# Turning filtered pieces to tokens with whole 128x128 transposes, and sorting chunks in the copies out

## The chip, the cores and the metric

The kernel runs on one core of one Trainium2 chip. The metric is the device time of one execution, in microseconds. The matrix engine (TensorE, PE in the profile) multiplies into eight PSUM banks of 2 KB per partition; ScalarE (ACT) and VectorE (DVE) read those banks; GpSimd (POOL) works on SBUF alone; SyncE (SP) only starts transfers here.

## The reference

The reference is one decoder layer: an attention-like block, a second block on the context, and a feed-forward block, each with a residual and a layer norm. The change lies in the first block, in two causal depthwise filters over the value stream, with 31 and 64 taps:

```python
v = jax.nn.silu(_dwconv_causal(hidden_states @ v_w.T, convv_w))
def fir(x, filt):
    y = _dwconv_causal(x.reshape(b, Ll, H * DV), filt.reshape(H * DV, -1))
    return y.reshape(b, Ll, H, DV)
short, long_, wide = (fir(v, fir_s), fir(v, fir_l), fir(v, fir_wd))
...
o = w_ctx[..., 0:1] * short + w_ctx[..., 1:2] * long_ + w_ctx[..., 2:3] * wide + w_ctx[..., 3:4] * delta_out + w_val * v
```

There are 4 sequences of 512 tokens and 256 channels. `delta_out` is a chunked delta rule: a 128x128 triangular inverse for each 128 tokens and two heads, then a recurrence over the four tiles of tokens. Everything is float32 in this part.

## The kernel before

The program is five stages, one after another. **Stage 2**, from 59.9 us to about 344.5 us of the profiled span, has the keys and queries, the inverse, the recurrence and both long filters. It is written by hand, engine by engine: each engine has its own queue in the order of the code, and waits for counters (semaphores) that the others raise.

**The filters** go over the 256 channels in 32 pieces of 8 channels. For one piece n:

- POOL copies the piece's values into `v_piece` (L1448).
- `filter_piece(n)` (L732) does 8 matmuls on PE, one for each channel: the values of 32 chunks (4 sequences of 8 chunks of 64 tokens) against a 128x128 table that holds both filters' taps. Two channel groups of 4 fill columns 0 to 255 of the piece's bank: partition = (channel of 4, chunk of 32), column = (filter, token of 64).
- ACT copies the bank's left half to SBUF, into `fir_s`, with the tokens turned round (`filter_out`, L1081, signal `windows_out`).
- `to_tokens(n)` (L745) brings tokens onto the partitions, on PE, with the result in columns 256 to 511 of the same bank.
- ACT copies that to `filtered` (`tokens_out`, L1086, signal `fir_out`), whose layout is partition = token within a tile of 128, then (filter, tile of 16, channel of 256). A piece has 8 neighbouring channels, so one tile is 1 KB from the next.

A tile of 128 tokens is two chunks: the one of even number belongs on partitions 0 to 63, the one of odd number on 64 to 127. Before the change `to_tokens` does this sorting itself: the constant `c_select` (128x128) picks the 16 tiles' even or odd chunks, in 8 small matmuls, for two groups of channels, two filters and two parities. One copy of 128x256 then suffices.

**Order around it.** PE runs `to_tokens(n - 1)` behind the 8 matmuls of `filter_piece(n)`. ACT's `filter_out(n)` is `tokens_out(n - 1)` and then the copy of piece n. `filter_piece(n + 1)` waits for the copy of piece n (`windows_out`) and for `fir_out` of piece n - 1. Pieces 0 to 7 lie in the **opening** of stage 2 (62 to 97 us), in one bank and between the steps that prepare sequence 0. After it, for each sequence b, comes `inverse(b)` (five rounds of products, no filter work) and `recurrence(b)`: seven pieces each for b = 0, 1, 2 (p0 to p6 below), three for b = 3. In `recurrence(b)` PE weaves the pieces between the steps of the recurrence and those that prepare sequence b + 1:

- turn_k (L756), updates (L692), next_state (L949), outputs (L967), piece p0, q_norms (L765), piece p1, turn_norms (L771)
- state_part (L927), p2, updates, p3, next_state, outputs (L964, L967)
- state_part, p4, updates, turn_back (L779), next_state, outputs, p5
- state_part, p6, updates, gram (L795, L799), to_tokens(p6), outputs; then `attend` (L819) opens `inverse(b + 1)` and waits for `fir_out` of p6.

ACT has in the same stretch, between its copies for pieces, `u_out` (L1154: PE's next_state waits for it), `square` (L1065), `k_back_out` (L1117: PE's gram waits for it) and `cross_out` (L1124).

Of the kernel before, what the change touches and what calls it, by code (L numbers as in the profile page):

```python
# [24 lines left out]
P = 128  # L25
B, L, D = 4, 512, 256
H, DK = 4, 64
# [3 lines left out]
NJ = L // DK  # L31
# [8 lines left out]
PIECE = 8  # L40
# [8 lines left out]
def shape_constants():  # L49

    i = np.arange(P)
    c = {}
    c["ident"] = np.eye(P)
    row, col = i[:, None] % DK, i[None, :] % DK
# [11 lines left out]
    for m in range(KT):  # L66
        heads[i, m, 12 + 2 * m + i // DK] = 1.0
    c["heads"] = heads
    sel = np.zeros((4, B, NJ, 2, 4, B, NJ // 2))
    for par in range(2):  # L70
        sel[:, :, par::2, par] = np.eye(4 * B * (NJ // 2)).reshape(4, B, NJ // 2, 4, B, NJ // 2)
    c["select"] = sel
    t = np.arange(HALF)
    f = np.arange(P)
    dft, inv = np.zeros((HALF, 4, P)), np.zeros((P, 4, HALF))
# [91 lines left out]
def layer(nc, dr, out):  # L167
    ctx = ExitStack()
    with ctx:
        def sb(name, shape, dt=F32):  # L170
            return ctx.enter_context(nc.sbuf_tensor(name, shape, dt))
# [16 lines left out]
        arena = sb("arena", [P, 30624])  # L188

        const_shapes = {n: a.shape[1] for n, a in shape_constants().items() if n not in LATE_CONST}  # L190
        const = {n: sb("c_" + n, [P, w]) for n, w in const_shapes.items()}
        ident = const["ident"]
# [20 lines left out]
        def stat_of(b, n, s):  # L213
# [38 lines left out]
        filtered = arena[:, 0:WL].rearrange("p (f t c) -> p f t c", f=2, c=D)  # L252
# [3 lines left out]
        A2 = carve(arena, {  # L256
            "xT": (KT, L), "kq": (2, 4, L), "k_tok": (2, TT, D), "v_sc": (TT, D),
            "above": (TT, 2, KT, DK), "cross": (TT, 2, KT, DK), "atT": (TT, 2, KT, P), "X": (TT, 2, KT, DK),
            "XT": (TT, 2, P), "Z": (2, 2, 4, DK // 2), "full": (TT, 2, KT, P),
            "S": (2, KT, P), "ss": (32,), "ks": (16,), "C": (16,), "root": (TT, H), "rn": (2, 2 * TT, H), "th": (16,),  # L260
            "v_piece": (2, PIECE, B * NJ), "fir_s": (4, DK)},
            at=WL + TOEP_BUFS * TOEP)
# [349 lines left out]
        fir_bank = lambda n: bank[5 if n < OPENING else 3]  # L612
# [11 lines left out]
        half = lambda a: slice(a * DK, (a + 1) * DK)  # L624
# [30 lines left out]
        with nc.Block() as block:  # L655
# [30 lines left out]
            def _(pe):  # L686
                mm = nc.tensor.matmul
# [50 lines left out]
                def to_tokens(n):  # L738

                    pe.wait_ge(s2["windows_out"].sem, n + 1)  # L740
                    for c4 in range(PIECE // 4):
                        for f in range(2):
                            for par in range(2):
                                col = D + f * P + c4 * DK
                                i = mm(fir_bank(n)[half(par), col:col + DK], A2["fir_s"][:, 2 * c4 + f, :],  # L745
                                       const["select"][:, half(par)], start=True, stop=True)
                    i.then_inc(s2["turn_mm"].sem, 1)

                def turn_k(b):
# [222 lines left out]
                def recurrence(b, more):  # L972
# [19 lines left out]
                    if more:  # L992
                        filter_piece(piece[3])
                    else:
                        to_tokens(piece[2])
# [19 lines left out]
                    if more:  # L1015
                        gram(b + 1, 0)
                        gram(b + 1, 1)
                        to_tokens(piece[6])
# [30 lines left out]
            def _(act):  # L1049
# [33 lines left out]

                def tokens_out(n):
                    act.wait_ge(s2["turn_mm"].sem, n + 1)
                    nc.scalar.copy(filtered[:, :, :, n * PIECE:(n + 1) * PIECE].rearrange("p f t c -> p f c t"),  # L1086
                                   fir_bank(n)[:, D:2 * D].rearrange("p (f c t) -> p f c t", f=2, c=PIECE))\
                        .then_inc(s2["fir_out"].sem, 1)

                def beta_rows_out(b):  # L1090
                    act.wait_ge(s2["beta_rows"].sem, s2["beta_rows"].at(b, 1))
# [1555 lines left out]
```

## Time and profile before

| | us |
|---|---|
| median of 3 executions | 709.68 (709.62 to 709.91) |
| the profiled execution, its own time | 705.24 |
| its span, first to last instruction | 703.4 |
| mean granted clock of TensorE over the span | 0.944 of 2.4 GHz |

| engine | busy us | share | instructions |
|---|---|---|---|
| PE matmul | 585.3 | 83% | 7436 |
| PE weight load | 426.2 | 61% | 7448 |
| DVE | 455.5 | 65% | 890 |
| ACT | 282.8 | 40% | 518 |
| POOL | 118.5 | 17% | 102 |

Busy is the union of an engine's instructions in time. One float32 matmul stands in the trace as two records, one float32 transpose as one. Instructions of one engine overlap: the second can start before the first has ended, so the distance between two starts is what an instruction takes from its engine, and its own duration is what one who waits for it sees. The profiled execution was 4.4 us shorter than the median of the timed ones; the span and what lies around it are 705.24 us.

### The profile page before, as it was taken

How to read it: one execution, taken by the hardware profiler on the slowest of the kernel's cores; microseconds unless marked ns; L12 is line 12 of the kernel's file. 1: busy time of each engine (PE TensorE's matmuls, PEld its weight loads, DVE VectorE, ACT ScalarE, POOL GpSimd, SP SyncE). 2: the span in 40 equal slices, each digit the busy share in tenths (PEclk: the TensorE clock that was granted, in tenths of full speed). 3: DMA queues.
4: the chain of work that ended last, by engine and by line, in shares of the span. 5: the costliest groups of instructions: out<-in, count | busy, mean ns of one | idle time of the engine just before them, and what ended most of it. 6: DMA issues, size and time to landing. Idle time of an engine off the chain costs nothing. (4 is left out here: it accounts for less than half of the span.)

```text
span 703.4 us, 16960 instructions
## 1 busy us (share of the span) xinstructions
PE 585.3 (83%) x7436; PEld 426.2 (61%) x7448; DVE 455.5 (65%) x890; ACT 282.8 (40%) x518; POOL 118.5 (17%) x102
## 2 busy tenths in 40 slices
PE   5868679899998999878696886599999767998984
PEld 2544466777767676776443545488888554555542
DVE  2963367857784786774818889664277774676674
ACT  1874634432453344323344253332323144554431
POOL 1001340250034006000011203434100020000000
PEclk9999899999999999998799998899999887999998
DMA  5501420340052004001510005400000000000001
GB/s 175 207 1 44 152 79 4 104 139 4 4 156 89 3 23 161 4 4 64 207 31 30 31 0 156 134 1 0 1 1 0 1 0 1 1 0 31 31 4 58
DMA packets 26537, 37.51 MB, mean 53 GB/s; under 512 B 4641, under 2 KB 13602, under 8 KB 26463
## 3 DMA queue, kind: packets, MB, share of 16 engines
q1 hardware_dynamic: 26463, 36.42, 16.0%
q8 instruction: 59, 0.97, 0.6%
q14 instruction: 15, 0.12, 0.1%
HBM read 34.31 MB, written 2.10 MB: 52 GB/s over the span
## 5 line engine op out<-in xcount | busy, mean ns | idle before, releaser
L298 DVE SCALAR_TENSOR_TENSOR arena<-bank,conv_w,arena 128x511 f32<-128x511 f32 (+2 forms) x72 | 53.2, 746 | 30.9 <-ACT arena L1070 15.5
L1448 POOL COPY arena<-v_win 128x256 f32<-128x256 f32 x32 | 21.1, 684 | 196.8 <-PE bank L732 196.8
L1898 ACT COPY arena<-bank 128x512 f32<-128x512 f32 x40 | 23.3, 584 | 57.1 <-PE bank L1701 36.8
L1701 PE MATMUL bank<-v_win,arena 128*128 128x256 f32 x192 | 45.6, 386 | 0.0
L2473 PE MATMUL bank<-v_win,arena 128*128 128x256 bf16 x288 | 36.5, 279 | 7.9 <-DVE arena L2560 6.9
L732 PE MATMUL bank<-arena 128*32 128x128 f32 x512 | 35.7, 409 | 8.1 <-ACT arena L1081 7.6
L1131 ACT COPY arena<-bank 128x512 f32<-128x512 f32 x40 | 21.6, 589 | 50.8 <-PE bank L854 50.8
L1086 ACT COPY arena<-bank 128x256 f32<-128x256 f32 x32 | 19.3, 602 | 53.9 <-PE bank L745 53.9
L1701 PEld LDWEIGHTS bank<-v_win,arena 128*128 128x128 f32 x192 | 37.1, 195 | 5.5 <-issue 0.4
L2473 PEld LDWEIGHTS bank<-v_win,arena 128*128 128x128 bf16 x288 | 28.4, 100 | 16.6 <-DVE arena L2560 7.9
L2463 PE MATMUL bank<-arena,v_win 128*128 128x512 bf16 x134 | 35.1, 390 | 3.7 <-DVE arena L2531 3.2
L1683 PE MATMUL bank<-v_win,arena 128*128 128x256 f32 x128 | 31.9, 409 | 5.9 <-DVE arena L2165 4.0
L2463 PE MATMUL bank<-arena 128*128 128x512 bf16 x142 | 35.5, 385 | 0.1
L1627 PE MATMUL bank<-arena 128*128 128x512 f32 x64 | 33.4, 649 | 0.0
L1683 PEld LDWEIGHTS bank<-v_win,arena 128*128 128x128 f32 x128 | 26.2, 207 | 10.6 <-issue 4.2
L839 PE MATMUL bank<-arena 64*64 64x32 f32 x1280 | 23.5, 221 | 9.3 <-DVE arena L1344 3.9
L705 PE MATMUL bank<-arena,qkv_w 128*128 128x512 f32 x64 | 30.2, 597 | 0.9 <-PEq L303 0.6
L865 PEld LDWEIGHTS bank<-arena 64*64 64x64 f32 x1280 | 21.7, 139 | 11.6 <-issue 11.1
L839 PEld LDWEIGHTS bank<-arena 64*64 64x64 f32 x1280 | 20.9, 134 | 12.0 <-DVE arena L1344 7.1
L2510 ACT CAST arena<-arena 128x512 bf16<-128x512 f32 x24 | 14.8, 618 | 31.7 <-DVE arena L2540 31.7
L732 PEld LDWEIGHTS bank<-arena 128*32 128x32 f32 x512 | 15.8, 122 | 18.8 <-issue 13.5
L745 PEld LDWEIGHTS bank<-c_select,arena 128*64 128x64 f32 x512 | 18.3, 142 | 14.6 <-issue 12.9
(275 smaller groups left out, 1355.4 us busy)
## 6 DMA issues: line engine op xcount, KB each, us to landing
arena<-in_toep_w SPq DMA_DIRECT2D x32, 256.0 KB, 3.0
arena<-in_toep_l SPq DMA_DIRECT2D x32, 256.0 KB, 3.7
arena<-in_xT SPq DMA_DIRECT2D x12, 512.0 KB, 4.6
arena<-in_x SPq DMA_DIRECT2D x4, 512.0 KB, 3.9
arena<-in_ctx SPq DMA_DIRECT2D x4, 512.0 KB, 4.4
out<-arena SPq DMA_DIRECT2D x4, 512.0 KB, 2.9
qkv_w<-in_qkv_wT SPq DMA_DIRECT2D x1, 768.0 KB, 5.4
v_win<-in_w_gateT SPq DMA_DIRECT2D x1, 768.0 KB, 4.9
```

The lines of the kernel that those rows point to most:

```text
L298: return nc.vector.scalar_tensor_tensor(out=acc[:, j:L], in0=src[:, 0:L - j], scalar=conv_w[:, m, CONV_K - 1 - j:CONV_K - j], in1=acc[:, j:L],
L705: i = mm(proj_bank(m)[:], qkv_w[:, k, m * P:(m + 1) * P], A2["xT"][:, k, :], start=(k == 0), stop=(k == KT - 1))
L732: i = mm(fir_bank(n)[32 * (c % 4):32 * (c % 4) + 32, (c // 4) * P:(c // 4 + 1) * P], A2["v_piece"][:, n % 2, c, :], toep[n % TOEP_BUFS][:, ...
L839: i = mm(zw_bank(th, a)[half(p), c:c + DK // 2], A2["above"][half(a), t, e, p, :], x, start=True, stop=True)
L865: i = mm(zw_bank(th, p)[half(a), c:c + DK // 2], A2["XT"][half(p), t, e, half(a)], A2["Z"][half(p), th, a, 2 * t2 + e, :], start=True, sto ...
L1131: nc.scalar.copy(A2["XT"][:, 2 * th:2 * th + 2, :, :], turn_bank(th)[:].rearrange("p (t e c) -> p t e c", t=2, e=2)).then_inc(s2["xt_out"] ...
L1627: mm(hid_bank(m)[:], g1x_w[:, k, m * P:(m + 1) * P], A3[b % 2]["xT"][:, k, :], start=(k == 0), stop=False)
L1683: i = mm(o[:, par * 256:(par + 1) * 256], src[:, par, k, d * P:(d + 1) * P], dft[:, k, par * 256:(par + 1) * 256], start=(k == 0), stop=(k ...
L1701: i = mm(oo, src[:, k, f * P:(f + 1) * P], w[:, k, :], start=(k == 0), stop=(k == KT - 1 and f > 0))
L1898: nc.scalar.copy(dst(i), bank[RING_FIRST + n % RING].rearrange("p (t c) -> p t c", c=dst(i).shape[-1]))\
L2463: i = mm(bank[first + n % 2][:], w[:, k, m * P:(m + 1) * P], parts[b % 2][part][:, k, :], start=(j == 0 and k == 0), stop=(j == 2 and k == ...
L2473: i = mm(bank[6 + t // 2][:, (t % 2) * D:(t % 2 + 1) * D], parts[b % 2][part][:, m, t * P:(t + 1) * P], wd[:, m, :], start=(m == 0 and j = ...
```

## The change

`to_tokens` does two transposes for a piece instead of eight matmuls with `c_select`: one for each group of four channels, of the whole 128x128 window (both filters, 64 tokens each). Its result has partition = (filter, token of 64) and column = (channel, tile, parity). The constant is gone, with its load. `tokens_out` now does the sorting: for each filter and each parity one copy from 64 partitions of the bank to 64 partitions of `filtered`, 8 channels by 16 tiles each, reading every second column. Only the last of the four raises `fir_out`.

```diff
@@ shape_constants
-    sel = np.zeros((4, B, NJ, 2, 4, B, NJ // 2))
-    for par in range(2):
-        sel[:, :, par::2, par] = np.eye(4 * B * (NJ // 2)).reshape(4, B, NJ // 2, 4, B, NJ // 2)
-    c["select"] = sel
@@ to_tokens
                     for c4 in range(PIECE // 4):
-                        for f in range(2):
-                            for par in range(2):
-                                col = D + f * P + c4 * DK
-                                i = mm(fir_bank(n)[half(par), col:col + DK], A2["fir_s"][:, 2 * c4 + f, :],
-                                       const["select"][:, half(par)], start=True, stop=True)
+                        i = nc.tensor.transpose(fir_bank(n)[:, D + c4 * P:D + (c4 + 1) * P],
+                                                A2["fir_s"][:, 2 * c4:2 * c4 + 2, :].rearrange("p f t -> p (f t)"), ident[:])
                     i.then_inc(s2["turn_mm"].sem, 1)
@@ tokens_out
-                    nc.scalar.copy(filtered[:, :, :, n * PIECE:(n + 1) * PIECE].rearrange("p f t c -> p f c t"),
-                                   fir_bank(n)[:, D:2 * D].rearrange("p (f c t) -> p f c t", f=2, c=PIECE))\
-                        .then_inc(s2["fir_out"].sem, 1)
+                    turned = fir_bank(n)[:, D:2 * D].rearrange("p (c t two) -> p c t two", c=PIECE, two=2)
+                    for f in range(2):
+                        for par in range(2):
+                            i = nc.scalar.copy(filtered[half(par), f, :, n * PIECE:(n + 1) * PIECE].rearrange("p t c -> p c t"),
+                                               turned[half(f), :, :, par])
+                    i.then_inc(s2["fir_out"].sem, 1)
```

No instruction changes its place in a queue; SP loses one transfer, and DVE and POOL keep their instructions. Lines after L69 have moved up, by 4 to 7 ahead of `tokens_out` and by 4 behind it. PE at the end of the opening, before: `filter_piece(6)`, its turn of piece 5 (L745), `filter_piece(7)`, the turns of pieces 6 and 7, and `attend` (L819).

```order
L732 MATMUL bank<-arena 32x128 x8
L745 MATMUL bank<-c_select,arena 64x64 x8
L732 MATMUL bank<-arena 32x128 x8
L745 MATMUL bank<-c_select,arena 64x64 x16
L819 MATMUL bank<-arena 128x128 x8
```

The same place on PE after, where L728 is the filter, L738 the turn and L812 `attend`:

```order
L728 MATMUL bank<-arena 32x128 x8
L738 MATMUL bank<-c_ident,arena 128x128 x2
L728 MATMUL bank<-arena 32x128 x8
L738 MATMUL bank<-c_ident,arena 128x128 x4
L812 MATMUL bank<-arena 128x128 x8
```

Each turn of a piece went from eight matmuls to two transposes, at the same places. ACT in `recurrence(0)`, before, from the turned piece p1 (L1086) to the copies of the scaled keys (L1117):

```order
L1086 COPY arena<-bank 128x2x8x16
L1081 COPY arena<-bank 128x256
L1154 COPY arena<-bank 128x256
L1086 COPY arena<-bank 128x2x8x16
L1081 COPY arena<-bank 128x256
L1065 ACTIVATE arena<-arena 128x1024
L1086 COPY arena<-bank 128x2x8x16
L1081 COPY arena<-bank 128x256
L1154 COPY arena<-bank 128x256
L1117 COPY arena<-bank 128x2x256 x2
```

The same place on ACT after; L1082 is the copy of the turned piece, L1074 that of the filtered one, L1150 is `u_out`, L1058 `square` and L1113 `k_back_out`:

```order
L1082 COPY arena<-bank 64x8x16 x4
L1074 COPY arena<-bank 128x256
L1150 COPY arena<-bank 128x256
L1082 COPY arena<-bank 64x8x16 x4
L1074 COPY arena<-bank 128x256
L1058 ACTIVATE arena<-arena 128x1024
L1082 COPY arena<-bank 64x8x16 x4
L1074 COPY arena<-bank 128x256
L1150 COPY arena<-bank 128x256
L1113 COPY arena<-bank 128x2x256 x2
```

Every copy of a turned piece became four in a row, of half the partitions and half the elements for each partition; what stands behind each is the same as before.

## Rows read from the trace of the kernel before

**Rows 1.** Group by line and shape, 80 to 420 us: busy us, mean ns, idle before.

```profile
L1086 ACT COPY arena<-bank 128x256 f32<-128x256 f32 x29 | 17.5, 603 | 51.9 <-PE bank L745 51.9
```

**Rows 2.** Groups of ACT by line and shape, whole span, same columns.

```profile
L1154 ACT COPY arena<-bank 128x256 f32<-128x256 f32 x16 | 6.0, 373 | 8.4 <-PE bank L692 8.4
...
L1124 ACT COPY arena<-bank 64x512 f32<-64x512 f32 x8 | 4.6, 577 | 12.6 <-DVE arena L1281 12.6
...
L482 ACT COPY arena<-bank 128x128 f32<-128x128 f32 x4 | 1.1, 265 | 3.6 <-PE bank L400 3.6
```

**Rows 3.** Timeline of ACT in stage 1: start us, duration us, instruction.

```profile
43.57 0.27 ACT L482 COPY arena<-bank 128x128 f32<-128x128 f32 x1
43.73 0.64 ACT L450 ACTIVATE arena<-arena 128x512 f32<-128x512 f32 x1
```

**Rows 4.** Timeline of all engines in `recurrence(1)`, around piece p3's turn.

```profile
209.45 0.69 PE L745 MATMUL bank<-c_select,arena 128*64 128x64 f32 x16
...
209.96 0.64 PE L692 MATMUL bank<-arena 128*64 128x64 f32 x16
210.18 0.63 ACT L1086 COPY arena<-bank 128x256 f32<-128x256 f32 x1 [2.32 <-PE bank L745]
...
210.53 1.09 PE L779 MATMUL bank<-c_ident,arena 128*128 128x128 f32 x8
210.60 0.42 ACT L1081 COPY arena<-bank 128x256 f32<-128x256 f32 x1
210.91 0.38 ACT L1154 COPY arena<-bank 128x256 f32<-128x256 f32 x1
...
211.46 0.61 PE L949 MATMUL bank<-arena 128*128 128x128 f32 x4
```

**Rows 5.** The same timeline: pieces p2, p3 and p6, then the end.

```profile
201.47 1.11 PE L732 MATMUL bank<-arena 128*32 128x128 f32 x16 [0.40 <-ACT arena L1081]
...
204.32 1.11 PE L732 MATMUL bank<-arena 128*32 128x128 f32 x16 [0.65 <-ACT arena L1081]
...
216.13 1.11 PE L732 MATMUL bank<-arena 128*32 128x128 f32 x16 [0.47 <-ACT arena L1081]
...
221.93 0.60 ACT L1086 COPY arena<-bank 128x256 f32<-128x256 f32 x1 [0.58 <-PE bank L745]
...
223.29 1.16 PE L819 MATMUL bank<-arena 64*128 64x128 f32 x16
```

**Rows 6.** Timeline of PE in the opening, where it waits for ACT.

```profile
80.40 1.08 PE L765 MATMUL bank<-arena,c_heads 128*32 128x128 f32 x16 [4.84 <-ACT arena L1112]
...
84.53 1.14 PE L732 MATMUL bank<-arena 128*32 128x128 f32 x16 [0.70 <-ACT arena L1081]
...
92.55 1.11 PE L732 MATMUL bank<-arena 128*32 128x128 f32 x16 [1.11 <-ACT arena L1081]
...
95.19 0.69 PE L745 MATMUL bank<-c_select,arena 128*64 128x64 f32 x16 [0.91 <-ACT arena L1081]
...
96.76 1.16 PE L819 MATMUL bank<-arena 64*128 64x128 f32 x16 [0.89 <-ACT arena L1086]
```

**Rows 7.** Timeline of PE in `recurrence(3)`, pieces p2 and its turn.

```profile
328.42 1.11 PE L732 MATMUL bank<-arena 128*32 128x128 f32 x16 [0.47 <-ACT arena L1081]
...
331.05 0.69 PE L745 MATMUL bank<-c_select,arena 128*64 128x64 f32 x16 [0.44 <-ACT arena L1081]
```

**Rows 8.** Windows: us, busy PE, PEld, DVE, ACT, POOL; clock; DMA share, GB/s.

```profile
40.00:48.00 8.00, 5.96 (x64) 4.67 (x54) 6.85 (x11) 6.10 (x15) 0.00 (x0) 1.00 0.01 2
...
94.00:96.00 2.00, 0.96 (x26) 0.68 (x22) 0.22 (x1) 1.37 (x4) 1.19 (x2) 1.00 0.58 150
78.00:80.00 2.00, 0.00 (x0) 0.00 (x0) 0.00 (x0) 2.00 (x6) 2.00 (x1) 0.50 0.87 294
```

**Rows 9.** Timeline of PE in `inverse(3)`, in a stretch of half clock.

```profile
305.18 1.16 PE L865 MATMUL bank<-arena 64*64 64x32 f32 x64 [0.33 <-ACT arena L1131]
...
310.90 1.93 PE L865 MATMUL bank<-arena 64*64 64x32 f32 x64
```

## The prediction

> **What bounds the kernel now.** The busy table is the first view: PE 83%, ACT 40%. That alone would say that a lighter PE and a heavier ACT must pay. But the turns of pieces stand only in stage 2's opening and recurrences, so I read who waits there, in the timeline. There PE is often the one that waits, and it waits for ACT: `filter_piece` for the copy of the piece before it by 0.40, 0.65 and 0.47 us in one recurrence [rows 5], by 0.70 and 1.11 us in the opening, where the turns themselves and `attend` wait for ACT too, by 0.91 and 0.89 us [rows 6], and in the last recurrence [rows 7]. Between these waits PE runs without a gap, and ACT waits for PE: 51.9 us in 29 waits before the copy of the turned piece [rows 1]. So this is a ring. PE's turn, ACT's copy of the turn, ACT's copy of the next piece, PE's next filter; each piece goes once round it. What counts is what the change takes from PE's part of the ring and what it adds to ACT's, not the shares.
>
> **PE's part, removed.** A turn takes 0.51 us from PE (209.45 to the next group's 209.96), and ACT starts its copy 0.73 us after the turn's start (210.18) [rows 4]. Whole transposes are in the same row group: the eight of L779 take from 210.53 to 211.46, 0.93 us, 0.117 each, and the first start to the last end is 1.09, so the last one lasts 0.27. Two take 0.23 us from PE and end after 0.117 + 0.27 = 0.39; ACT starts 0.04 behind the end of a turn now (210.18 against 209.45 + 0.69), so 0.43 after the start. **PE's next work is 0.28 us earlier, ACT's copy 0.30 us.**
>
> **ACT's part, added.** The one copy of 128x256 lasts 0.603 us [rows 1]; a plain copy of that shape lasts 0.373, one of 128x128 lasts 0.265 [rows 2]. That is 0.84 ns for each element of a partition and 0.157 fixed. The other 0.23 us, 0.9 ns per element, must come from its writes, each 1 KB from the last, since its reads are plain. The next copy starts 0.40-0.42 after it and ends late too: 0.42 against 0.38 for the L1154 behind it [rows 4]. The four new copies write in the same way, 128 elements each, together 512 elements for each lane where there were 256. Half the partitions save nothing: 64x512 lasts 0.577 [rows 2], on the line of 0.157 + 512 x 0.84 = 0.587.
>
> What the four cost ACT is not in the trace, so I bound it. Let **x** be the time by which everything behind them on ACT comes later, counted from their start. From below: a plain 128x128 copy lets the next begin after 0.16 us [rows 3]; four are 0.64, against 0.40 now: x = 0.24. Below zero is excluded, because twice the elements per lane can't be copied in less. From above: four without any overlap, each 0.265 + 128 x 0.9 ns = 0.38, are 1.52: x = 1.12. The nearest rows lie between. Twice the present pace, four times 0.20 us, gives x = 0.40. The write pace, 512 elements at 1.73 ns against 256, gives 0.44, and with three joints of 0.04 (0.16 less 128 x 0.84 ns is 0.05) 0.56. I take **x = 0.48**, the middle of 0.40 and 0.56, because both are the same scattered writes. `fir_out` comes 3 x 0.22 + 0.38 = 1.04 after the start, where it was 0.60: 0.44 later, less the 0.30.
>
> What no row shows is the read of every second column. By the Trainium skill's SBUF page ("SBUF — State Buffer", Door 1: The DMA port swizzle) PSUM is read in lines of 8 bytes and SBUF in lines of 16, and each change of line is paid for. The reversed read of L1081 costs little; a step of 8 bytes is not in the trace. If that read were the slower side, the case is the first rival below.
>
> **The opening, pieces 0 to 7.** Each term is followed to the place where PE waits. ACT reaches the copies of q's squares, for which PE waits 4.84 us, as a row of its own work: the copies for pieces 1 and 2 lie in it, once with PE ahead by 0.58 and a wait of 0.16 us on PE absorbed: 2x - 0.74 = +0.22. The turn behind that is at half clock and saves about 0.45; F(5) waits for the next copy: 3x - 1.19 = +0.25. Then each piece adds x - 0.30 = 0.18: F(6) and the grams ahead of it +0.43, F(7) +0.61, the last turn +0.79. `attend` waits for the turned piece's copy: 0.79 - 0.30 + 0.44 = 0.93. **Opening: +0.9 us.** The wait behind each of these is already ACT's [rows 6], so nothing covers them.
>
> **A recurrence of seven pieces.** p2's filter waits for ACT: x - 0.30 = +0.18. p3's: +0.36. next_state behind p2's turn is PE's own pace again: 0.36 - 0.28 = +0.08. p3's turn: `u_out` comes 0.08 - 0.30 + 0.48 = +0.26 later, and next_state starts at 211.46, some 0.11 us after it needs to (210.91 + 0.38 and 0.06 to react [rows 4]): +0.15. p5's filter follows, p6's waits for ACT: 0.15 - 0.30 + 0.48 = +0.33. Then two turns on PE with no wait for ACT between them, updates and grams behind the first and outputs behind the second: 0.33 - 0.28 - 0.28 = -0.23. `attend` waits for the last copy, which ended at 222.53, 0.76 before `attend` started [rows 5]; it ends 0.05 - 0.30 + 0.44 = +0.19 later, still hidden. **-0.23 us each, -0.7 in three.** Without the cover of those 0.76 us it would be +0.19. In general one is 4x - 2.15, so it turns from gain to loss at x = 0.54. The DVE work that opens the next inverse waits for the outputs and goes with them.
>
> **The last recurrence.** Two waits for ACT [rows 7], the first turn at half clock: (x - 0.45) + (x - 0.30) - 0.28 = **-0.1**; after it DVE's reductions follow the outputs. The missing 64 KB load lies among the first loads, whose data are not needed until later: nothing. Stages 3 to 5 start when stage 2 ends, so its shift is the kernel's.
>
> **Sum:** +0.9 - 0.7 - 0.1 = +0.1 us. On the profiled execution, 705.24, that is 705.4; on the median of the timed runs, which is 4.4 us more throughout, 709.68 + 0.1 = **709.8 us**. The sum is about 21x - 10 (7x from the opening, 12x from three recurrences, 2x from the last), so 0.1 us of x is 2.1 us of time. 0.2% is 1.4 us, about what a measurement of this kernel can tell from no change.
>
> **Rivals.**
>
> 1. *ACT takes over the ring: slower.* If the strided read, or a pause between copies, makes x over 0.55, every wait of PE for ACT grows and PE's savings are only idle time. For it: ACT already ends the wait at four places of the opening and three of each recurrence [rows 5, 6]. Against it: overlapping is what every pair of ACT rows shows. At x = 0.65 it is 21 x 0.17 = +3.6: **713.4**. At the upper bound of 1.12 it would be 13 us. Chance 0.28.
>
> 2. *The scattered writes hide in the overlap: faster.* Four copies at the plain pace with a little more, x = 0.30, give -3.8: **705.9**. For it: the next copy starts 0.20 us before the scattered one ends. Against it: that next copy ends late. Chance 0.22.
>
> 3. *The clock falls.* The granted clock fell to half (1.2 GHz) when PE had stood idle from 75.6 us on [rows 6, 8]; at 94 to 96 us PE is busy for 0.96 of 2 us and it holds. There PE will stand longer. If it fell there, the first products of `inverse(0)` would run at 1.93 instead of 1.16 us for a group of 64 records [rows 9]; two such and the transposes beside them are about 2 us: **711.9**. Chance 0.07. By the Trainium skill ("TensorE: Matmul & The Clock Gate", Part 4: PE-mode transpose) a transpose does not count as busy for the clock, which would make this likelier. The trace speaks against it: from 40 to 48 us most of PE's records are stage 1's transposes of the values, and the clock is 1.00 [rows 8].
>
> That the change doesn't do what it says can be left out: the order of both engines shows the new instructions at the old places.
>
> **How the numbers follow.** My forecast, within 1.4 us of before, has 0.43; the rivals 0.28, 0.22 and 0.07. The range reaches from x = 0.34 (-3.0) to x = 0.68 (+4.2): **706.7 to 713.9**. Faster by over 0.2% 0.22, within it 0.43, slower 0.35.
>
> **What would show it.** Two records of about 0.27 us per turn, and ACT's copy 0.43 us behind the turn's start: PE's part right. ACT's starts from the first of four to the copy of the next piece: 0.88 is x = 0.48; over 0.95 is rival 1, under 0.75 rival 2. Start of `attend` in the opening later by 0.9; a recurrence, from its first updates to `attend`, shorter by 0.2. PE's waits for L1074 larger than those for L1081 were, each by about 0.2 more than the one before. The forecast is wrong altogether if the copies' durations differ from 0.38 by much, or if the stretches at half clock lie elsewhere than at 78 to 85, 310 to 313 and 320 to 327 us.

## The result, and the profile after

| | us | before, measured beside it |
|---|---|---|
| median of 4 executions | 720.53 (717.49 to 725.77) | 709.65 (709.34 to 709.91) |
| the profiled execution | 725.77 | 705.24 |
| its span | 724.0 | 703.4 |
| mean granted clock | 0.924 | 0.944 |

The ratio is 1.0161, with a 95% interval of 1.0099 to 1.0223: the change made the kernel slower by 1.0 to 2.2%, 10.9 us by the medians. The forecast was 709.8, with a range to 713.9. It is the case that the prediction had at the upper bound of its first rival, 13 us.

The page of the kernel after, busy time of each engine:

```profile
PE 589.3 (81%) x7000; PEld 423.6 (59%) x7000; DVE 455.6 (63%) x890; ACT 315.7 (44%) x614; POOL 118.5 (16%) x102
```

ACT has 33 us more, PE 4 us more with 436 fewer records (more of its time at half clock). Both together say little about 20 us of span. The page's groups of instructions say more; the columns are busy us, mean ns of one, idle time before them and what ended it:

```profile
L1082 ACT COPY arena<-bank 64x128 f32<-64x128 f32 x128 | 47.9, 374 | 44.4 <-PE bank L738 43.3
...
L728 PE MATMUL bank<-arena 128*32 128x128 f32 x512 | 35.7, 409 | 22.4 <-ACT arena L1074 21.9
```

The copy of a turned piece was one of 603 ns [rows 1]; it is four of 374 ns. And the filter (L728) now waits 21.9 us for the copy of the piece before it. In the kernel before, the list of PE's waits has 7.6 us for the same pair of lines:

```profile
PE bank L732 <- ACT arena L1081: 7.6, 13, 1.1
```

The same list of the kernel after (us in total, times, longest):

```profile
PE bank L728 <- ACT arena L1074: 21.9, 14, 2.2
...
PE bank L758 <- ACT arena L1108: 6.2, 1, 6.2
...
PE bank L812 <- ACT arena L1082: 4.5, 4, 1.8
PE bank L942 <- ACT arena L1150: 4.4, 8, 0.7
```

`attend` (L812) waited once for the turned piece before the change, 0.89 us [rows 6]; now it waits in front of each of the four inverses. next_state (L942) waits for `u_out` eight times, 4.4 us, where it waited five times, 2.4 us. The number of the filter's waits is nearly the same, 14 against 13. They are three times as long: no new wait arose there, the old one grew.

The timeline of PE and ACT in `recurrence(1)` after, at full clock, pieces p2 to p4 (start us, duration us, instruction, idle time before it):

```profile
219.53 1.11 PE L728 MATMUL bank<-arena 128*32 128x128 f32 x16 [1.50 <-ACT arena L1074]
220.57 0.44 PE L738 MATMUL bank<-c_ident,arena 128*128 128x128 f32 x2
...
220.94 0.69 PE L688 MATMUL bank<-arena 128*64 128x64 f32 x16
221.05 1.52 ACT L1082 COPY arena<-bank 64x128 f32<-64x128 f32 x4 [0.81 <-PE bank L738]
222.60 0.37 ACT L1074 COPY arena<-bank 128x256 f32<-128x256 f32 x1
222.87 0.38 ACT L1150 COPY arena<-bank 128x256 f32<-128x256 f32 x1
223.22 1.11 PE L728 MATMUL bank<-arena 128*32 128x128 f32 x16 [1.60 <-ACT arena L1074]
```

Read it as the ring of the prediction. PE's turn starts at 220.57, ACT's four copies at 221.05. They take until 222.57. The copy of the next piece starts at 222.60, 1.55 us after the first of the four. It was 0.42 us after it before (210.18 to 210.60, [rows 4]). PE's next filter follows at 223.22. Between the four copies there is no overlap at all: 4 x 0.374 is 1.50, and the row's 1.52 to 1.56 us is that with a few ns between each two. Record by record, each of the four starts about 12 ns after the end of the one before, and the copy behind them 24 ns after. By the prediction's measure, x = 1.17 (1.57, the usual distance, less 0.40).

**Where the time went, part by part.** I cut each profiled span at the first product of stage 2 on PE, at the starts of `attend`, and at the first updates of each recurrence. `inverse` is from `attend` to the first updates, `recurrence` from there to the next `attend`, the last one to VectorE's first instruction of stage 3. All in us; in brackets how much of it had the clock at half.

| part | before | after | e3, one copy | e2, runs | e7, before + runs |
|---|---|---|---|---|---|
| stage 1 | 59.9 (3.4) | 63.1 (10.2) | 62.4 (10.2) | 57.7 (0) | 62.0 (6.8) |
| opening | 36.9 (6.8) | 45.0 (19.8) | 34.8 (6.8) | 39.6 (13.7) | 35.9 (6.8) |
| inverse(0) | 33.5 (0) | 36.9 (7.5) | 35.0 (3.4) | 36.6 (6.8) | 33.5 (0) |
| recurrence(0) | 29.4 | 32.9 (3.4) | 26.5 | 29.4 | 27.7 |
| inverse(1) | 34.5 | 33.5 | 34.3 | 33.8 | 34.5 |
| recurrence(1) | 29.1 | 31.8 | 26.5 | 29.4 | 28.9 |
| inverse(2) | 34.5 | 33.5 | 34.3 | 33.8 | 34.5 |
| recurrence(2) | 28.2 | 32.9 (3.4) | 26.5 | 29.4 | 27.7 |
| inverse(3) | 33.5 (3.4) | 30.0 (0) | 30.4 | 29.9 | 33.1 (3.4) |
| recurrence(3) | 25.1 (10.6) | 25.9 (7.6) | 22.7 (7.3) | 23.8 (3.9) | 23.2 (3.4) |
| the rest | 358.9 | 358.5 | 358.7 | 358.7 | 358.1 |

The three right columns are experiments, told below. From before to after: opening +8.1, inverse(0) +3.4, the recurrences +3.5, +2.7, +4.7 and +0.8, inverse(3) -3.5. Stage 1, whose instructions are the same in both, has +3.2: its stretches at half clock differ from one execution to the next. The profiled execution was also the slowest of the four.

The opening has a second cause beside the ring. Windows of the kernel after (columns as in [rows 8], the clock is the number after the busy times):

```profile
81.00:88.00 7.00, 2.39 (x34) 1.78 (x35) 1.00 (x6) 4.49 (x10) 3.80 (x3) 0.53 0.37 116
...
92.00:98.00 6.00, 5.21 (x105) 4.80 (x103) 1.44 (x3) 2.84 (x7) 5.92 (x3) 0.50 0.27 90
...
102.00:115.00 13.00, 9.22 (x118) 7.36 (x117) 2.05 (x5) 5.04 (x13) 0.62 (x1) 0.50 0.13 47
```

Before, the clock was at half for 6.8 us of the opening and at full through `inverse(0)`. Now it falls to half (1.2 GHz) three times, each time after PE has stood for ACT. The rows in front of the falls, PE's timeline:

```profile
85.61 1.08 PE L758 MATMUL bank<-arena,c_heads 128*32 128x128 f32 x16 [6.23 <-ACT arena L1108]
...
90.42 1.11 PE L728 MATMUL bank<-arena 128*32 128x128 f32 x16 [2.01 <-ACT arena L1074]
...
101.87 0.44 PE L728 MATMUL bank<-arena 128*32 128x128 f32 x4 [2.24 <-ACT arena L1074]
```

### The profile page after: what moved, and what is told of

The parts are those of the page before. It is cut to its first block and busy times, and to the rows that moved or that the text cites. A ratio compares the mean times of both kernels' runs of the same rounds, so it can differ in the third digit from the quotient of the medians.

```text
span 724.0 us, 16171 instructions
## 1 busy us (share of the span) xinstructions
PE 589.3 (81%) x7000; PEld 423.6 (59%) x7000; DVE 455.6 (63%) x890; ACT 315.7 (44%) x614; POOL 118.5 (16%) x102
## 5 line engine op out<-in xcount | busy, mean ns | idle before, releaser
L1082 ACT COPY arena<-bank 64x128 f32<-64x128 f32 x128 | 47.9, 374 | 44.4 <-PE bank L738 43.3
L728 PE MATMUL bank<-arena 128*32 128x128 f32 x512 | 35.7, 409 | 22.4 <-ACT arena L1074 21.9
L1894 ACT COPY arena<-bank 128x512 f32<-128x512 f32 x40 | 23.3, 585 | 56.9 <-PE bank L1697 36.7
L1679 PE MATMUL bank<-v_win,arena 128*128 128x256 f32 x128 | 31.8, 408 | 6.1 <-DVE arena L2161 4.1
L728 PEld LDWEIGHTS bank<-arena 128*32 128x32 f32 x512 | 15.9, 122 | 33.4 <-issue 28.3
L701 PE MATMUL bank<-arena,qkv_w 128*128 128x512 f32 x64 | 30.1, 595 | 0.9 <-PEq L299 0.6
L2506 ACT CAST arena<-arena 128x512 bf16<-128x512 f32 x24 | 14.8, 618 | 31.6 <-DVE arena L2536 31.6
L354 PE MATMUL bank<-arena,qkv_w 128*128 128x512 f32 x32 | 19.5, 753 | 9.8 <-DMA c_ident<-in_c_ident 7.6
```

Of the source, the lines that this page charges most:

```text
L701: i = mm(proj_bank(m)[:], qkv_w[:, k, m * P:(m + 1) * P], A2["xT"][:, k, :], start=(k == 0), stop=(k == KT - 1))
L728: i = mm(fir_bank(n)[32 * (c % 4):32 * (c % 4) + 32, (c // 4) * P:(c // 4 + 1) * P], A2["v_piece"][:, n % 2, c, :], toep[n % TOEP_BUFS][:, ...
L1082: i = nc.scalar.copy(filtered[half(par), f, :, n * PIECE:(n + 1) * PIECE].rearrange("p t c -> p c t"), turned[half(f), :, :, par])
L1679: i = mm(o[:, par * 256:(par + 1) * 256], src[:, par, k, d * P:(d + 1) * P], dft[:, k, par * 256:(par + 1) * 256], start=(k == 0), stop=(k ...
L1894: nc.scalar.copy(dst(i), bank[RING_FIRST + n % RING].rearrange("p (t c) -> p t c", c=dst(i).shape[-1]))\
L2506: nc.scalar.copy(parts[u]["h_hi"][:, m, :], A5[u]["h"][:, m % 2, :]).then_inc(s5["h_split"].sem, 1)
```

## The experiments

The four copies differ from the one in several ways at once: they read every second column, they write in the same scattered way but twice as many elements per lane, and they go from one partition half to another. So three theories on why x is 1.17 stood beside each other. **Read**: the step in the bank costs. **Write**: the scattered writes cost, 1 KB apart. **Half**: a copy on other partitions than the one before it can't begin until that one has ended. What each predicts stands in the quoted text of each experiment. The ratio given is to the kernel before, measured beside it. Each kernel's profile is of one execution.

**e1: contiguous reads.** POOL puts even and odd chunks apart in `v_piece`, so the turned columns of a parity lie side by side (POOL's side of the edit is left out here):

```diff
-turned = fir_bank(n)[:, D:2 * D].rearrange("p (c t two) -> p c t two", c=PIECE, two=2)
+turned = fir_bank(n)[:, D:2 * D].rearrange("p (c two t) -> p c two t", c=PIECE, two=2)
```

> The changed kernel with one thing else: GpSimd writes the 32 chunks of a channel in the order (parity, tile) instead of (tile, parity), so that each of ScalarE's four copies reads 16 neighbouring columns of the bank and not every second one. Same result, same four copies, same scattered writes. Theory R (the read of every second column keeps the copies from overlapping): the four starts move from 0.385 us apart to about 0.2, the distance from the first to the copy of the next piece from 1.57 to about 0.9 us, the time from 720.5 to about 710. Theory W (the writes, 1 KB apart, do it) and theory I (four instructions on half the partitions, whatever they read, do it): 1.57 us and about 720 as before.

721.93 us, ratio 1.0195 (1.014 to 1.0251), not told apart from the change itself; 14.8 us over before by the medians. The group of the four copies, in e1:

```profile
L1082 ACT COPY arena<-bank 64x128 f32<-64x128 f32 x128 | 47.9, 374 | 44.8 <-PE bank L738 43.7
```

47.9 us and 374 ns, to the digit what it was. The read step costs nothing, and the theory of the read falls. The prediction had weighed it by the Trainium skill ("SBUF — State Buffer", Door 1: The DMA port swizzle: PSUM read in lines of 8 bytes, each change of line paid for): for ACT's copies out of PSUM these runs show no such price at a step of 8 bytes.

**e2: writes in runs.** The same four copies with the loops of the copy exchanged. It writes the 8 channels of a tile side by side and reads them 128 bytes apart:

```diff
-i = nc.scalar.copy(filtered[half(par), f, :, n * PIECE:(n + 1) * PIECE].rearrange("p t c -> p c t"),
-                   turned[half(f), :, :, par])
+i = nc.scalar.copy(filtered[half(par), f, :, n * PIECE:(n + 1) * PIECE],
+                   turned[half(f), :, :, par].rearrange("p c t -> p t c"))
```

> The changed kernel with each of the four copies going over its elements in the other order: channel innermost, so that it writes runs of 8 neighbouring values (32 bytes) and reads with a step of 32 columns (128 bytes). Same result. Theory W: a copy takes 0.27 us instead of 0.37 and the next begins after 0.16 to 0.2; the distance from the first to the next piece's copy falls to 0.65 to 0.85 us, the time to 704 to 710. Theory R: the reads are as strided as before, 1.57 us and about 720 stay. Theory I: starts stay as far apart as a copy lasts, whatever that is; with 0.27 us a copy 1.1 us and about 713.

706.54 us, ratio 0.9989 (0.9959 to 1.0018). The order of two loops is worth 15 us here, against e1, measured beside it. Group, and one place in e2's timeline of ACT:

```profile
L1082 ACT COPY arena<-bank 64x128 f32<-64x128 f32 x128 | 33.3, 260 | 43.6 <-PE bank L738 42.5
```

```profile
221.74 1.08 ACT L1082 COPY arena<-bank 64x128 f32<-64x128 f32 x4 [1.77 <-PE bank L738]
222.84 0.37 ACT L1074 COPY arena<-bank 128x256 f32<-128x256 f32 x1
```

A copy takes 260 ns, the 265 of a plain one [rows 2]; 114 ns for 128 elements is 0.9 ns each, the prediction's figure. The writes are the price, and reads 128 bytes apart cost nothing either. But the four still don't overlap: 4 x 0.260 = 1.04 in 1.08, and the next after 1.10. After a plain copy of 128x128 the next instruction began 0.16 us later [rows 3]. So more than half of the trouble is left: x = 0.70.

**e3: one copy.** Transposes on PE as in the change, and one copy of the old shape. It leaves out the sorting of chunks into partition halves.

> The changed kernel's two transposes a piece, but ScalarE's one copy of 128x256 of the kernel before; the sorting of chunks into the partition halves is left out. It prices the TensorE part alone. By the prediction's sum, with x = 0: 21 x 0 - 10, about 700; the ring model of the prediction gives at least -5 us. If TensorE's part were idle time in any case (the rival that PE gains nothing): 709 to 710.

695.23 us, ratio 0.9837 (0.9798 to 0.9876). Timeline of ACT in `recurrence(1)` of e3:

```profile
207.84 0.63 ACT L1079 COPY arena<-bank 128x256 f32<-128x256 f32 x1 [1.87 <-PE bank L738]
208.26 0.44 ACT L1074 COPY arena<-bank 128x256 f32<-128x256 f32 x1
```

0.42 between the starts, as before. This is x = 0, where the prediction's sum says -10 us; the run says -11.9 (3.1 of it in `inverse(3)`, which the sum does not hold and which comes below). So PE's transposes bring about what was counted for them, and all that is lost is lost in the copies.

**e9: two full copies.** The same amount of scattered writing on all 128 partitions, in two copies of 128x128; it leaves out the layout that the later steps need.

```diff
-for f in range(2):
-    for par in range(2):
...
+for par in range(2):
+    i = nc.scalar.copy(filtered[:, par, :, n * PIECE:(n + 1) * PIECE].rearrange("p t c -> p c t"),
+                       turned[:, :, :, par])
```

> The changed kernel with two copies of all 128 partitions and 128 elements each (one for each parity) in place of four of 64 partitions; the move between partition halves is left out, so chunks of both parities lie in the wrong place. Reads of every second column and scattered writes stay. Theory H (half the partitions is what stops the overlap): the second starts about 0.2 to 0.3 us after the first, and the next piece's copy some 0.4 to 0.5 us after it starts; x is about 0.0 to 0.1 and the time about 697. Theory N (ScalarE copies with scattered writes of 128 elements don't overlap whatever their partitions): 0.385 us apart, 0.77 to the next piece's copy, x = 0.37, about 702.

693.67 us (one execution; before 708.46). ACT in `recurrence(1)` of e9:

```profile
214.16 0.62 ACT L1081 COPY arena<-bank 128x128 f32<-128x128 f32 x2 [1.78 <-PE bank L738]
214.56 0.42 ACT L1074 COPY arena<-bank 128x256 f32<-128x256 f32 x1
```

The two are 405 ns each by their group (64 of them), together 0.81, and lie in 0.62 us; the next starts 0.40 after the first. So splitting a copy costs nothing, scattered writes overlap well, and reading every second column changes nothing. What is left is the half.

**e4: four copies, old matmuls.** The kernel before with its one copy split in four, each from one half to the same half, the filter in the outer loop:

```diff
+turned = fir_bank(n)[:, D:2 * D].rearrange("p (f c t) -> p f c t", f=2, c=PIECE)
+for f in range(2):
+    for par in range(2):
+        i = nc.scalar.copy(filtered[half(par), f, :, n * PIECE:(n + 1) * PIECE].rearrange("p t c -> p c t"),
+                           turned[half(par), f, :, :])
```

> The kernel before, with its eight matmuls, but its one copy of 128x256 cut into four of 64x128: for each filter and each partition half, from a half to the same half, 16 neighbouring columns at a time, writes scattered as before. Same result. It prices the four copies alone. Theory R: starts about 0.2 us apart, 0.9 us to the next piece's copy, about 8 to 10 us slower than before (718 to 720). Theory W: 0.37 to 0.385 us apart, 1.57 us, 730 or more. Theory I: the same as W. Against each other W and I are told apart by the run with writes in runs.

734.81 us, ratio 1.0385 (1.0341 to 1.0428). 373 ns each, 12 ns between them: the change's copies without the transposes, and the worst kernel of all. Its `recurrence(1)` is 33.9 us against 31.8 after: PE's part of the ring is worth 2.1 us there, and was forecast as 2.15.

**e5: the same, half by half.** Only the two loops are exchanged, so two neighbouring copies have the same half:

```diff
-for f in range(2):
-    for par in range(2):
+for par in range(2):
+    for f in range(2):
```

> The run with the old matmuls and four copies of 64x128, with the copies in another order: both filters of the lower partition half first, then both of the upper, so that the first and second, and the third and fourth, stay on one half. Theory H1 (a copy on half the partitions never lets the next begin before it ends): all starts 0.385 us apart, as with the other order, median about 735. Theory H2 (only a change of the half between two copies stops the overlap): the first and third distance fall to about 0.2 us, the other stays, the group gets 0.35 us shorter and the time about 7 us.

728.51 us (one execution). Group and timeline of ACT in e5:

```profile
L1089 ACT COPY arena<-bank 64x128 f32<-64x128 f32 x128 | 38.0, 395 | 50.1 <-PE bank L745 49.8
```

```profile
218.41 1.19 ACT L1089 COPY arena<-bank 64x128 f32<-64x128 f32 x4 [1.07 <-PE bank L745]
219.63 0.37 ACT L1081 COPY arena<-bank 128x256 f32<-128x256 f32 x1
```

Four of 0.395 are 1.58, and they take 1.19: the two pairs overlap by 0.2 us each, and at the change of half there is a pause of 12 ns. The same four shapes, the same writes, only in another order. This settles the theory of the half, by the distances in the trace; the time, of one execution, agrees with it. The copy of all 128 partitions behind them also waits for the end (219.60 to 219.63).

**e7: the kernel before, with writes in runs.** If the writes cost 0.9 ns per element, the old kernel pays too:

```diff
-nc.scalar.copy(filtered[:, :, :, n * PIECE:(n + 1) * PIECE].rearrange("p f t c -> p f c t"),
-               fir_bank(n)[:, D:2 * D].rearrange("p (f c t) -> p f c t", f=2, c=PIECE))\
+nc.scalar.copy(filtered[:, :, :, n * PIECE:(n + 1) * PIECE],
+               fir_bank(n)[:, D:2 * D].rearrange("p (f c t) -> p f t c", f=2, c=PIECE))\
```

> The kernel before, with its one copy of the turned piece going channel by channel innermost, so that it writes runs of 8 values (32 bytes) and reads with a step of 64 bytes. Same result. Theory W for the scattered write: the copy lasts 0.37 to 0.38 us instead of 0.60 and the next piece's copy starts after 0.31 instead of 0.40, x = -0.09; by the ring model about 1.5 to 2 us less than before. If a copy's reads with a step cost as much as its writes do: no change.

703.56 us, ratio 0.9941 (0.991 to 0.9973): faster than both kernels. The group in e7, to be held against [rows 1]:

```profile
L1086 ACT COPY arena<-bank 128x256 f32<-128x256 f32 x32 | 11.9, 372 | 53.3 <-PE bank L745 53.3
```

603 ns became 372, the next copy starts 0.27 instead of 0.40 us later, and PE's wait for L1081 falls from 7.6 to 4.2 us. The gain is small for a copy 231 ns shorter, since the scattered writes were already overlapped by 0.2 us.

**e8: e2 with two banks in the opening.** The turns of pieces 0 to 7 go to a bank of their own (bank 4, unused there), and ACT copies the filtered piece ahead of the turned one. PE then doesn't wait for the four copies in its next filter; the next turn waits for them in its place:

```diff
+tok_bank = lambda n: bank[4 if n < OPENING else 3]
...
-if behind > 0:
+if behind > 0 and n >= OPENING:
     pe.wait_ge(s2["fir_out"].sem, behind)
...
+if 0 < n < OPENING:
+    pe.wait_ge(s2["fir_out"].sem, n)
...
+if 0 < n < OPENING:
+    act.wait_ge(s2["turn_mm"].sem, n)
...
+if not first and n < OPENING:
+    tokens_out(n - 1)
```

> The run with transposes and writes in runs, and in the opening alone the turned pieces go to a bank of their own (4; it is free there), with ScalarE copying the next filtered piece out before the turned one. So TensorE's next filter no longer waits for the four copies. Ring theory: the waits of the filter for L1074 in the opening shrink from about 1.3 us each to the order of 0.3, the opening gets some 3 to 5 us shorter, the kernel some 3 to 5 us faster than the run without it (about 702). If the opening is bound by something else (the loads of the filters' tables, the chain of q's norms): under 1 us.

701.66 us, ratio 0.9936 (0.9904 to 0.9968). Opening 36.7 us (6.8 at half clock) instead of e2's 39.6 (13.7), and `inverse(0)` 33.5 (0) instead of 36.6 (6.8). Windows of e8:

```profile
78.00:98.00 20.00, 12.51 (x267) 8.85 (x270) 7.21 (x12) 10.72 (x34) 12.45 (x8) 0.84 0.38 123
98.00:118.00 20.00, 18.86 (x567) 14.26 (x564) 15.27 (x35) 7.40 (x13) 0.00 (x0) 1.00 0.01 3
```

In this execution the clock holds at 1.00 through `inverse(0)`. In the kernel after 102 to 115 us had 0.50. That doesn't show that the waits make the clock fall: not all of them are gone (the last turn still waits 1.58 us for L1089 and `attend` 1.36), and e11 below has nearly the same waits and a fallen clock. Of e8's gain over e2, 3.1 us in `inverse(0)` and a part of the opening's 2.9 are the clock's.

**e10: which side's half?** e2 with the order of e5: two neighbours write the same half and read different ones.

> The run with transposes and writes in runs (median 706.5), with the four copies in the order upper half for both filters, then lower half for both: within a pair the half that is written stays and the half that is read changes; the last pair writes the lower half, before the full-width copy of the next piece. Theory D (only a change of the written half stops the overlap): the first and third distance fall from 0.272 to about 0.17 us, the distance from the first to the next piece's copy from 1.10 to 0.9; x falls by 0.2 and by the ring model the time by 3 to 4 us. If in addition a full-width copy may overlap one on the lower half: another 0.1 us and 2 us. Theory E (a change of either half stops it): no distance changes, the time stays at the one without.

707.8 us, ratio 1.0034 (1.0005 to 1.0064), no gain over e2. ACT in `recurrence(1)` of e10:

```profile
227.41 1.08 ACT L1082 COPY arena<-bank 64x128 f32<-64x128 f32 x4 [1.77 <-PE bank L738]
228.50 0.37 ACT L1074 COPY arena<-bank 128x256 f32<-128x256 f32 x1
```

Again 1.08 for four, with pauses of 12 ns. In e5 both sides stayed on their half and overlapped; here the written side stays, the read side changes, and it doesn't. Either side is enough. With sources in two halves and targets in two halves, no order of the four avoids it: that is the cost of sorting in the copies.

**e11: e8 and e10 together.**

> All that helped on the changed kernel: writes in runs, upper half first, and in the opening a bank of its own for the turned pieces with the filtered piece copied out first. Ring model: the run with two banks (ratio 0.9936 to before) less what the order of copies gives in the recurrences, 2 to 3 us under theory D: ratio about 0.990. Under theory E 0.9936.

706.44 us, ratio 0.9996 (0.9972 to 1.0019): the gain of e8 isn't there. In the opening of e8 the full copy (L1079) is followed by a copy from the lower to the lower half, which starts 0.27 us after it, 0.10 before its end. In e11 a copy to the upper half follows and starts 24 ns after the end. Such joints are too small for 4.8 us. Most of the loss is the clock's. Windows of e11, over the same stretches as those of e8 above:

```profile
78.00:98.00 20.00, 10.82 (x195) 7.06 (x195) 6.88 (x13) 12.81 (x38) 13.46 (x8) 0.79 0.46 150
98.00:118.00 20.00, 19.03 (x448) 15.33 (x448) 11.69 (x26) 5.15 (x9) 0.00 (x0) 0.79 0.01 3
```

From 96.4 us on, 10.2 us are at half clock, where e8 has none, and the opening and `inverse(0)` together are 4.1 us longer than in e8. The waits in front of that fall are 1.71 and 1.37 us, in e8 1.58 and 1.36. It isn't one odd execution: the mean granted clock of an execution has a median of 0.939 in e11 and 0.946 in e8. Why the clock falls in one of them and holds in the other stays open. The two were also timed apart, against before at 708.46 (e8) and 706.38 (e11).

**e12: e7 with two banks.** The old matmuls with e8's edit for the opening.

> The kernel before, with its one copy writing in runs (ratio 0.9941 alone) and the opening's turned pieces in a bank of their own. In the opening, TensorE's filter no longer waits for the copy of the turned piece (0.31 us each, three to five waits) and keeps its longer turns: 1 to 2 us less than with the runs alone, ratio about 0.992. If it comes out below the run with all changes on the transposes, the transposes are worth nothing beside the simple change of the writes' order.

702.04 us, ratio 0.994 (0.9905 to 0.9974), as e7. With copies of 0.37 us the waits in the opening are small, and the second bank finds little to take away.

Three versions beat the kernel before by some 0.6%: e7, e8 and e12. They are not told apart. e7 is the simplest, one line in the old kernel. The comparison of transposes with matmuls under equal writes, e2 against e7, reads 0.9989 and 0.9941, with intervals that overlap; with two banks, e8 against e12, it reads 0.9936 and 0.994. So sorting in the copies (x = 0.70) takes back at least about what the transposes give PE, and no run shows a gain from the transposes over e7.

## Why the prediction was wrong

**What held.** The ring was the right picture, and so was its arithmetic. It says 4x - 2.15 for a recurrence, and its terms add up to 7x - 2.46 for the opening. Put in the x that each kernel shows (measured numbers are differences from the before column of the table):

| kernel | x measured | recurrence(1): by the formula | measured | opening: by the formula | measured |
|---|---|---|---|---|---|
| e3 | 0 | -2.15 | -2.6 | -2.5 | -2.1 |
| e2 | 0.70 | +0.65 | +0.3 | +2.4 | +2.7 |
| after | 1.17 | +2.5 | +2.7 | +5.7 | +8.1 |

`recurrence(1)` is the one at full clock in every column. The other two spread around it: in e3 -2.9 and -1.7, in e2 0.0 and +1.2, and in the kernel after +3.5 and +4.7, each with 3.4 us at half clock.

At x = 1.17 the whole sum, 21x - 10, would be +14.6. The medians say +10.9, and +14.8 for e1, whose copies have the same pace. The way the forecast was made would have come close, had x been right.

**The step that failed: x.** "The nearest rows lie between" took 0.48 for it, the middle of 0.40 and 0.56. The copy's own duration was forecast as 0.38 and is 0.374. x was 1.17. What was wrong was the overlap: I let four copies on changing halves overlap as pairs of full ones do, "because both are the same scattered writes". The argument against rival 1 was that "overlapping is what every pair of ACT rows shows". Of the two causes that rival 1 named it was the pause between copies, not the strided read (e1). And overlapping wasn't what every pair shows: the trace of the kernel before had rows without it. Two places, timeline of ACT:

```profile
126.67 0.58 ACT L1146 COPY arena<-bank 64x512 f32<-64x512 f32 x1 [0.93 <-PE bank L886]
127.28 0.27 ACT L1092 COPY arena<-bank 128x128 f32<-128x128 f32 x1
```

```profile
284.36 0.58 ACT L1124 COPY arena<-bank 64x512 f32<-64x512 f32 x1 [1.79 <-DVE arena L1281]
284.85 0.59 ACT L1086 COPY arena<-bank 128x256 f32<-128x256 f32 x1
```

Both are a copy of 64 partitions and then one of 128. L1146 works on partitions 64 to 127 (`[DK:P]` in the code); the next starts 0.03 us after its end. L1124 works on 0 to 63 (`[0:DK]`); the next starts 0.09 before its end. The width doesn't matter, the first partition does. I had taken the pace of the new copies from full ones. The pairs that had the new feature, a change of half, were five in the trace: three behind L1146 (126.67, 190.57 and 254.15) and two in a later stage (542.15 and 543.35), each with the next start about 25 ns after the end, and I hadn't looked for them. With them the upper bound, "four without any overlap", would have been the value: 1.12, and 12 to 13 us.

**PE's part** was nearly right. The turn's group ends 0.44 after its start and ACT follows 0.48 after it (220.57 to 221.05), where 0.43 was forecast, so 0.25 is gained instead of 0.30. PE's next group starts 0.27 to 0.40 after the turn, where 0.23 was forecast.

**The late end of `attend`** was priced as hidden behind a cover of 0.76 us, 0.19 by x = 0.48. At 1.17 it isn't: L812 waits four times, 4.5 us. Part of it costs nothing, since `inverse(1)` and `inverse(2)` are 1.0 us shorter after: DVE's masks, for which the inverse waits next, were no later, and PE's three waits for them in the inverses (L1284, 2.2 us before) are gone.

**Rival 3, the clock**, came true beside rival 1. The prediction gave 0.07 for it and priced it alone, though a large x lengthens the very waits after which it fell. That longer waits can bring the fall is borne out by the old matmuls: with waits of 0.6 to 1.1 us at the end of the opening (before, e7, e12) the clock holds there, with waits of 1.5 to 2.2 us (e5, e4) it is at half for 6.8 and 10.3 us. But they aren't all of it, as far as one profiled execution of each kernel tells. PE in e3, at the end of the opening:

```profile
93.50 1.11 PE L728 MATMUL bank<-arena 128*32 128x128 f32 x16 [1.10 <-ACT arena L1074]
...
95.89 0.44 PE L738 MATMUL bank<-c_ident,arena 128*128 128x128 f32 x2 [0.91 <-ACT arena L1074]
97.21 1.87 PE L812 MATMUL bank<-arena 64*128 64x128 f32 x16 [0.88 <-ACT arena L1079]
```

These are the waits of the kernel before, 1.11, 0.91 and 0.89 us [rows 6], and yet the clock fell: the products of `attend` take 1.87 us instead of 1.16. e3 has 3.4 us at half clock there and e9, with the same waits, 6.8. Of the eight kernels with transposes only e8 has none there. So the transposes seem to bring the fall nearer, beside the waits; which part each has, no run separates. The row that the prediction set against a part of the transposes in it, 40 to 48 us at full clock [rows 8], stands as read but did not carry over to the opening. The formula's opening is +5.7 and the measured one +8.1 with `inverse(0)` another +3.4; so about 6 us of the profiled execution are an estimate for the clock. The figure of 2 us for rival 3 had counted two groups at half clock; it was 13 us of them. The place was right, 94 to 98 us and `inverse(0)`.

**What I hadn't priced at all** is `inverse(3)`, 3.5 us shorter. Before, PE stood there for nothing that the profile shows, and then ran at half clock (timeline of PE, `inverse(3)`, before):

```profile
306.44 1.04 PE L839 MATMUL bank<-arena 64*64 64x32 f32 x56
309.22 0.32 PE L839 MATMUL bank<-arena 64*64 64x32 f32 x8 [1.74 <-issue]
```

After, the same products run as one group:

```profile
324.57 1.14 PE L832 MATMUL bank<-arena 64*64 64x32 f32 x64 [0.68 <-DVE arena L1340]
```

All eight kernels with transposes lack that pause and have `inverse(3)` at 29.8 to 30.4 us; all five with the old matmuls (before, e4, e5, e7, e12) have it at the same eight products, 0.7 to 1.7 us, and are at 32.5 to 35.3. So it goes with the instructions on PE. That the pause is PE's instruction supply is only argued.

**The chances.** Rival 1 had 0.28, but was weighed near its threshold (x = 0.65, 713.4), and the range ended at x = 0.68, though the text held 1.12 for possible. The bound should have been in the range, since nothing but a pattern seen on other copies spoke against it.

## What to carry to other kernels

When one instruction becomes several, don't price them by their durations and the usual overlap: look in the trace for pairs that change what the new ones change (partition half, source, shape), and read the distance between their starts. Where no such pair is found, the case without any overlap belongs in the range. And write in runs: in these copies between two layouts, ACT read with steps of 8, 64 and 128 bytes for nothing and paid 0.9 ns an element for writes 1 KB apart, so let the loops follow the target.

## What the runs showed of the hardware

- **ACT begins the next copy before the end of the last one only if neither the read nor the written side moves to another partition half.** Full to full 0.1 us before the end, 0.2 with scattered writes; same half to same half 0.19 to 0.22 (e5, scattered writes); lower half to full 0.09 (284.36 above) and full to lower half 0.10 (e8). With a change on one side or both: 12 ns after the end, 24 ns where it waits on a semaphore (after, e2, e4, e10), and the same from the upper half to full. A changed read didn't count where the next instruction reads SBUF and not a bank: in the opening of e11 the last of the four reads the bank's upper half and writes the lower, and the silu behind it (L1071), which reads SBUF from partition 0, starts 0.10 before its end, in both places where they meet, while a copy out of a bank starts 24 ns after it. The Trainium skill ("ScalarE: Activation LUTs", What ACT_TABLE_LOAD costs) says that ACTIVATEs back to back overlap by about 93 ns; the pairs with the same first partition and plain writes agree with it (0.09 to 0.10 us), those with scattered writes overlap by more, and those with a change of half do not overlap.
- **Scattered writes of ACT to SBUF, 1 KB apart, cost 0.9 ns for each element of a partition**: 602 against 372 ns for 256 elements (e7), 374 against 260 for 128 (e2). Steps of 8 and of 128 bytes on the PSUM side cost nothing (e1, e2).
- **A clock that falls costs far from where it fell.** In the kernel after it fell at 101.9 us, behind a wait of 2.24 us, and stayed at 1.2 GHz for 13 us, half of them in `inverse(0)`, where PE has no wait for these copies. With the old matmuls it fell there behind waits of 1.5 to 2.2 us (e4, e5) and not behind 0.6 to 1.1 (before, e7, e12); with transposes also behind 0.9 to 1.1 us (e3, e9). With the second bank it held in e8 and fell in e11.
